# Row-maximum scores from the high part of q alone, as pairs of 64-row matmuls

## What is computed

```
q = einsum('dc,bct->btd', Wq, init) + bq        # init = context, d = 64 channels
k = einsum('dc,bct->bdt', Wk, init) + bk
R = einsum('btd,bds->bts', q, k)                # 1024 queries x 1024 keys
attention = softmax(R)                          # over the keys
v = einsum('oc,bct->bto', Wv, x) + bv
out = einsum('bts,bsc->bct', attention, v)
x = x + out                                     # x is layer-normed on its way in
```

## Time and profile before

| | |
|---|---|
| median of 3 runs | 2455.48 us (2455.11 to 2458.72) |
| profiled execution: span of its instructions | 2449.9 us |
| the median over that span (launch and end, and the spread of runs) | 5.6 us |
| TensorE matmuls busy | 2257.1 us (92%) |
| VectorE busy | 1900.4 us (78%) |
| ScalarE busy | 1128.1 us (46%) |
| GpSimd busy | 837.1 us (34%) |
| mean granted TensorE clock | 0.980 |
| HBM read and written | 81.74 MB and 16.78 MB, 40 GB/s |

### The profile page before, as it was taken

The page is one execution under the profiler, slowest core; times in us unless marked ns, Lnnn a source line. Parts: engine busy times, 40 slices in busy tenths (PEclk is TensorE's granted clock), DMA queues, the critical chain, the costliest instruction groups (busy, mean ns, idle before and its releaser), DMA issues.

```text
span 2449.9 us, 34700 instructions
## 1 busy us (share of the span) xinstructions
PE 2257.1 (92%) x11359; PEld 1749.3 (71%) x11359; DVE 1900.4 (78%) x2972; ACT 1128.1 (46%) x1657; POOL 837.1 (34%) x520
## 2 busy tenths in 40 slices
PE   0997999999999999999999999999999999999986
PEld 0775777777777777777777777777777777777764
DVE  1437788888888888888888888888888888888873
ACT  1104444555554544555554544545554544555541
POOL 0003333344344333344344333344344333334430
PEclk7999999999999999999999999999999999999996
DMA  8001011011011011011011011011011011011000
GB/s 230 9 1 52 18 44 39 30 43 43 26 43 43 34 43 43 26 43 43 26 43 43 34 43 43 26 43 43 26 43 43 36 41 43 26 43 43 30 22 26
DMA packets 45417, 98.86 MB, mean 40 GB/s; under 512 B 13968, under 2 KB 22544, under 8 KB 45392
## 3 DMA queue, kind: packets, MB, share of 16 engines
q1 hardware_dynamic: 33504, 96.48, 11.3%
q10 hardware_dynamic: 11888, 2.05, 0.5%
HBM read 81.74 MB, written 16.78 MB: 40 GB/s over the span
## 4 chain that ended last, share of the span: by engine, by line
PE 65%; DVE 14%; issue 10%; ACT 3%; POOL 0%; DVEq 0%; ACTq 0%; DMA 0%; SPq 0%; POOLq 0%
PE acc L1056 9%; PE acc L1095 8%; PE shared L1014 6%; PE scores L1039 5%; DVE p_lo L900 5%; DVE c_hi L924 3%; PE shared L1227 2%; PE acc L1052 2%; PE acc L1053 2%; PE shared L1164 2%; PE acc L1054 2%; PE shared L1112 2%; PE scores L1026 2%; PE shared L1180 2%; PE scores L1192 2%
## 5 line engine op out<-in xcount | busy, mean ns | idle before, releaser
L634 POOL TENSOR_TENSOR p_sum<-p_sum,prob 128x1024 f32<-128x1024 f32 x192 | 506.2, 2636 | 127.7 <-ACT prob L698 121.9
L900 DVE TENSOR_TENSOR p_lo<-prob,p_hi 128x1024 fp32r<-128x1024 f32 x256 | 353.4, 1381 | 83.8 <-ACT p_hi L705 82.3
L793 DVE TENSOR_REDUCE neg_max<-scores 128x1 f32<-128x1024 f32 x256 | 312.0, 1219 | 72.8 <-PE scores L1039 70.9
L615 POOL TENSOR_TENSOR rstd<-var_eps,minus_half 128x1 f32<-128x1 f32 x128 | 127.2, 994 | 665.4 <-DVE var_eps L787 662.1
L698 ACT ACTIVATE prob<-scores 128x1024 f32<-128x1024 f32 x256 | 260.3, 1017 | 199.8 <-PE scores L1084 180.6
L705 ACT ACTIVATE p_hi<-prob 128x1024 fp32r<-128x1024 f32 x256 | 271.2, 1059 | 76.4 <-PE acc L1095 72.3
L631 POOL TENSOR_TENSOR p_sum<-prob 128x1024 f32<-128x1024 f32 x32 | 85.7, 2677 | 642.5 <-ACT prob L698 642.5
L1095 PE MATMUL acc<-p_hi,v_hi 128*128 128x512 f32 x512 | 176.6, 426 | 94.6 <-DVE p_lo L900 94.6
L1056 PE MATMUL acc<-m_whole,cT_whole 128*128 128x512 f32 x512 | 255.2, 600 | 0.0
L1039 PE MATMUL scores<-k_hh,q_hl 128*128 128x512 f32 x512 | 212.5, 496 | 0.2 <-DVE k_l L802 0.2
L1069 PE MATMUL shared<-signT,y_hi 128*128 128x512 f32 x512 | 206.5, 403 | 0.4 <-ACT oscale L687 0.4
(11 more groups left out here) (230 smaller groups left out, 4873.4 us busy)
## 6 DMA issues: line engine op xcount, KB each, us to landing
c_in<-in_ctx SPq DMA_DIRECT2D x32, 512.0 KB, 3.3
xn<-in_x SPq DMA_DIRECT2D x32, 512.0 KB, 4.1
x<-in_x SPq DMA_DIRECT2D x32, 512.0 KB, 3.3
c_val<-in_ctx SPq DMA_DIRECT2D x32, 512.0 KB, 3.5
out_x<-oscale SPq DMA_DIRECT2D x32, 512.0 KB, 2.9
wq_nat<-in_L_xattn_Wq SPq DMA_DIRECT2D x4, 1024.0 KB, 10.2
wf_first<-in_L_ffn_weight SPq DMA_DIRECT2D x1, 2048.0 KB, 17.9
m_whole<-in_L_ffn_weight SPq DMA_DIRECT2D x1, 2048.0 KB, 22.8
```

The lines of the kernel that those rows point to most:

```text
L634: nc.gpsimd.tensor_tensor(p_sum[:, :], p_sum[:, :], prob[s % 2][:, :], ALU.add).then_inc(p_summed, 1)
L793: nc.vector.tensor_reduce(neg_max[:, DQK + t:DQK + t + 1], scores[(t + 1) % 2][:, :], AX_X, ALU.max, negate=True).then_inc(row_max, 1)
L900: nc.vector.tensor_tensor(p_lo[s % 2][:, :], prob[s % 2][:, :], p_hi[s % 2][:, :].bitcast(F32), ALU.subtract).then_inc(p_lo_ready, 1)
```

## The change

The row-maximum scores are now q high times k high alone. The term q low times k high is left out of them; the scores of the exponentials (L1083, L1084) keep all their parts. With 64 channels that product has 64 rows. The pair of a tile is laid out so that the left keys (half 0) come from partitions 0-63, with `q_hl`, and the right keys (half 1) from partitions 64-127, with a new `q_m`, whose partitions 64-127 hold the high part of q. In the built program the first matmul has a tile of 64 rows and 128 columns at array position (0, 0), the second one at (64, 0). All other matmuls of the loop keep tiles of 128 rows. For this, `q_m` and `k_l1` have 128 partitions: the maxima and the ones in 0-7, zeros in 8-63, and q high and k low in 64-127. The transpose L1135 turns 8 columns, which makes it a tile of 128 rows and 32 columns. Each matmul of a pair now increments the semaphore, and the maximum waits for both. Line numbers after L776 grow by three or less.

```diff
-        q_hm = sb("q_hm", [DQK + T, D], F32R)
+        q_m = sb("q_m", [P, D], F32R)
-        k_l1 = sb("k_l1", [DQK + T, D], F32R)
+        k_l1 = sb("k_l1", [P, D], F32R)
-        neg_max = sb("neg_max", [P, DQK + T])
+        neg_max = sb("neg_max", [P, T])
...
-                            nc.scalar.activation(q_hm[0:DQK, half(h)], scores[0][0:DQK, half(h)], ACT.Identity,
-                                                 bias=bq_col[0:DQK, :]).then_inc(q_hi_ready, 1)
+                            nc.scalar.activation(q_m[DQK:P, half(h)], scores[0][DQK:P, half(h)], ACT.Identity,
+                                                 bias=bq_col[DQK:P, :]).then_inc(q_hi_ready, 1)
...
-                nc.vector.memset(k_l1[DQK:DQK + T, :].bitcast(F32), 1.0).then_inc(const_made, 1)
-                nc.vector.memset(neg_max[:, :], 0.0).then_inc(const_made, 1)
+                nc.vector.memset(k_l1[0:DQK, :].bitcast(F32), 0.0).then_inc(const_made, 1)
+                nc.vector.memset(q_m[0:DQK, :].bitcast(F32), 0.0).then_inc(const_made, 1)
                 nc.vector.memset(route3[:, :].bitcast(F32), 0.0).then_inc(const_made, 1)
                 dve.wait_ge(const_made, 3)
+                nc.vector.memset(k_l1[0:T, :].bitcast(F32), 1.0).then_inc(const_made, 1)
+                dve.wait_ge(const_made, 4)
...
-                    dve.wait_ge(maxscores_done, nth(8, a, t + 1))
+                    dve.wait_ge(maxscores_done, nth(16, a, 2 * t + 2))
...
-                    nc.vector.scalar_tensor_tensor(k_l1[0:DQK, half(h)], scores[1][0:DQK, half(h)], bk_col[0:DQK, :],
+                    nc.vector.scalar_tensor_tensor(k_l1[DQK:P, half(h)], scores[1][DQK:P, half(h)], bk_col[DQK:P, :],
...
-                    for h in range(2):
-                        last = mm(scores[(t + 1) % 2][:, half(h)], q_hl[:, t * P:(t + 1) * P], k_hh[:, half(h)], start=True, stop=True)
-                    last.then_inc(maxscores_done, 1)
+                    rows = (slice(0, DQK), slice(DQK, P))
+                    for h, q in enumerate((q_hl, q_m)):
+                        mm(scores[(t + 1) % 2][:, half(h)], q[rows[h], t * P:(t + 1) * P], k_hh[rows[h], half(h)],
+                           start=True, stop=True).then_inc(maxscores_done, 1)
...
-                        last = mm(scores[s % 2][:, half(h)], k_l1[:, s * P:(s + 1) * P], q_hm[:, half(h)], start=False, stop=True)
+                        last = mm(scores[s % 2][:, half(h)], k_l1[:, s * P:(s + 1) * P], q_m[:, half(h)], start=False, stop=True)
...
-                        nc.tensor.transpose(scores[0][0:DQK + T, 0:P], neg_max[:, 0:DQK + T], ident[:, :]).then_inc(max_turned, 1)
+                        nc.tensor.transpose(scores[0][0:T, 0:P], neg_max[:, :], ident[:, :]).then_inc(max_turned, 1)
```

More of the change, by code:

```diff
@@ L789, in row_maximum @@
                 def row_maximum(a, t):
-                    dve.wait_ge(maxscores_done, nth(8, a, t + 1))
+                    dve.wait_ge(maxscores_done, nth(16, a, 2 * t + 2))
                     dve.wait_ge(max_turned, nth(1, a - 1, 1))
-                    nc.vector.tensor_reduce(neg_max[:, DQK + t:DQK + t + 1], scores[(t + 1) % 2][:, :], AX_X, ALU.max,
+                    nc.vector.tensor_reduce(neg_max[:, t:t + 1], scores[(t + 1) % 2][:, :], AX_X, ALU.max,
                                             negate=True).then_inc(row_max, 1)
@@ L801, in key_remainder @@
                     dve.wait_ge(k_hi_ready, nth(2, b, h + 1))
-                    nc.vector.scalar_tensor_tensor(k_l1[0:DQK, half(h)], scores[1][0:DQK, half(h)], bk_col[0:DQK, :],
-                                                   k_hh[0:DQK, half(h)].bitcast(F32), ALU.add,
+                    nc.vector.scalar_tensor_tensor(k_l1[DQK:P, half(h)], scores[1][DQK:P, half(h)], bk_col[DQK:P, :],
+                                                   k_hh[DQK:P, half(h)].bitcast(F32), ALU.add,
                                                    ALU.subtract).then_inc(k_ready, 1)
@@ L882, in body @@
                             nc.vector.tensor_tensor(
-                                q_hm[DQK:DQK + T, half(h)].rearrange("r (t j) -> r t j", t=4),
-                                scores[0][DQK:DQK + T, 0:P].unsqueeze(1).to_broadcast([T, 4, P]),
-                                ident[DQK:DQK + T, DQK + 4 * h:DQK + 4 * h + 4].unsqueeze(2).to_broadcast([T, 4, P]),
+                                q_m[0:T, half(h)].rearrange("r (t j) -> r t j", t=4),
+                                scores[0][0:T, 0:P].unsqueeze(1).to_broadcast([T, 4, P]),
+                                ident[0:T, 4 * h:4 * h + 4].unsqueeze(2).to_broadcast([T, 4, P]),
                                 ALU.mult).then_inc(max_ready, 1)
@@ L1007, in _ @@
                 mm = nc.tensor.matmul
-                pe.wait_ge(const_made, 3)
+                pe.wait_ge(const_made, 4)
                 def transposes(h, src, semaphore):
```

## The result

The changed kernel takes 2509.06 us in the median of four runs (2507.89 to 2515.74), the kernel before 2455.38 us. The ratio is 1.0221, with a 95% interval of 1.0207 to 1.0236: slower by 53.7 us. The profiled execution is the run of 2515.74 us, with a span of 2513.9 us, 64.0 us over the 2449.9 us of before.

The account below looks back on a forecast made before the run. TensorE was taken to bound the kernel, busy throughout the 17.53 us row-maximum stage. 256 pairs x 0.15 us gave 38.4 us, all on the path and everything else at nothing: 2455.5 became 2494 us, range 2412 to 2522.

Parts of the forecast that it names:

- the likeliest case: Row-maximum stage: pairs side by side, TensorE drained at each mode change; +0.15 us a pair, 2494 us, chance 0.45.
- the changes of mode: L1039 pairs: going from 128-row to 64-row matmuls and back costs 0.15 us net per pair, 38.4 us for 256.
- The pair runs side by side.: L1039: two 64-row matmuls on different array rows run concurrently; the second costs nothing at best, 0.234 us at worst.
- Emptying at a change of mode.: Around each L1039 pair: next weight load starts 0.07 us before the recorded end, 0.33 us after a matmul's start.
- The open loads.: Around each L1039 pair: weight loads not hidden at mode changes, taken as 0.10 us each.
- the distance over a pair should be 0.85 us: Sign in the later profile: from the matmul before an L1039 pair to the one behind, 0.85 us against 0.70 before.
- All of it on the path.: Row-maximum stage has no slack: all 38.4 us lengthen the run, 1.2 us an iteration; VectorE only idles more.
- the free rival: Row-maximum stage: mode changes free, pairs side by side, VectorE then sets the end; 40 us faster, 2415, chance 0.25.
- Everything else is priced at nothing.: ScalarE's q_m and VectorE's k_l1 writes, L1084's 128 rows, L1135's 8 columns, extra increments and hidden memsets cost nothing.
- The second stretch of the earlier trace: Exponentials and weighting of the values, after the row-maximum stage: forecast unchanged at 31.0 us.
- The rule of the Trainium skill on tiling modes: L1039 pairs: changing the tiling mode, not just the tile, drains TensorE; two drains per pair, speaking against the change.

Follow-up runs that it names:

- layout alone: Changed kernel with 128-row matmuls for the row maxima again, new layout and both increments kept: 2463.86 us against 2458.69 for the kernel before, ratio 1.0028.

## Why the prediction was right, and where it was not

The direction, the mechanism and the range held: 2494 us forecast, 2509 measured, within 2412 to 2522 and also within the likeliest case's own 2480 to 2522. The loss of 53.7 us comes apart into 1.19 x 32 = 38 us for the changes of mode, where 38.4 were forecast, 0.24 x 31 = 7 us for the copies and the wait, and some 8 us that are left, which I put down to the clock. The last two terms the forecast did not have; that they fit into its range is luck. With the clock's fall and the counted wait removed the program takes 2493.96 us. That this equals the forecast to 0.1 us is partly chance: some 3 us for ScalarE's copies, which the forecast priced at nothing, are still in it.

- *The pair runs side by side.* Taken as the bound without a row, and right: both start within 0.01 us, and putting them on the same rows costs 0.22 us per pair.
- *Emptying at a change of mode.* The setup rows gave 0.07 us before the recorded end; the loop shows 0.08. From the matmul ahead to the pair's load it is 0.32 us, forecast 0.33.
- *The open loads.* Counted at 0.10 us each, with both loads of the pair at once. From the pair to the next load it is 0.43 us as worked out. The stage grew by 1.11 us; the emptying ahead of its first pair lies in the rest, and with it the eight pairs cost 1.19 / 8 = 0.149 us each, where 0.15 was forecast. One sign of the forecast was misread: "the distance over a pair should be 0.85 us" is 0.74 us from start to start. The records of the pair and of the matmul behind it begin with their open loads, so the last 0.10 us shows behind that start and not ahead of it.
- *All of it on the path.* Right: TensorE is busy for the whole stage, and VectorE only idles longer. The end of the stage was TensorE's; the free rival, in which VectorE sets it, needed changes of mode that cost nothing. Grouping showed its idea from the other side: with pairs two at a time TensorE did wait for VectorE within the stage.
- *"Everything else is priced at nothing."* This step failed. It holds for the memsets, the 128-row second operand, the column tile of L1138 and the increment on TensorE. It does not hold for the copies to partitions from 64 on (0.13 us more between starts, of which 0.11 to 0.14 us an iteration reaches the path) nor for the wait that counts by 16 (0.16 us ahead of one p_lo per iteration). With the emptying ahead of the first pair (0.08 us), which belongs to the changes of mode, they make the 0.32 us of the rest, 10 us in all; taken one by one they come to a little more. The second stretch of the earlier trace rows was unchanged, as forecast: up to there TensorE's instructions lie where they lay, within 0.1 us; all of this comes behind it, in a part of the iteration for which I had forecast nothing. I had looked at shapes and counts, not at how the neighbours overlap.
- *The clock.* The granted clock was 1.00 in the stretch before, and the forecast kept it there without a word. It fell at the fourth pair in 11 iterations of the profiled run, 16.5 us, and by their mean clock in fewer in the others. This is a term that the forecast lacked. The Trainium skill, TensorE: Matmul & The Clock Gate, Part 1, says that activity releases the throttle and that its lack brings it back. The trace agrees as to the level, 0.51 of full speed in the stretch shown, but TensorE is recorded busy in all of the stretches before it. The stretches before the fall hold the short router matmuls and the pairs with their emptyings; with 128-row pairs in the same order it did not fall, and moving one unit removed it. Which of the two weighs how much was not separated, and with other orders the clock fell without 64-row pairs.
- *The rule of the Trainium skill on tiling modes* (TensorEngine Tiling (Array Packing), Key Properties) held for the number of rows: at a change the next load began only 0.08 us before the recorded end, and a second pair in the same mode did not pay again. For the number of columns the setup rows had disagreed with it, and behind L1138, whose column tile changes, the next matmul starts after 0.03 us as it does behind L1135.

## What to carry to other kernels

Two 64-row matmuls side by side save one matmul's time (0.234 us with 512 columns here), and going into 64-row mode and out again costs about 0.37 us: two emptyings of 0.08 to 0.09 us and two weight loads of 0.10 us that nothing hides. So a lone pair between 128-row matmuls loses 0.14 us. Two pairs in a row gain 0.10 by this count, and 0.13 us was measured at the group that waited for nothing; over a whole stage of four groups only 0.05 us came of it (17.73 against 17.78 us), since one group waited for VectorE. Longer runs in one mode were not tried. Price a change of operand layout by the starts of the neighbouring instructions, and after every change look at the granted clock per stage: moving one unit of the changed kernel was worth some 10 us, and another order of the kernel before cost 60 us, 33 of them by the clock.

## What the runs showed that I had not expected

- ScalarE's copies of equal length start 0.57 us apart when all begin at partition 0, and 0.70 us apart when every second one begins at partition 64.
- The form of a counted wait can cost the engine 0.16 us elsewhere in its program: with a count of 8 per batch p_lo starts 0.18 us behind the reciprocal, with 16 per batch 0.34 us, in each of the thirteen kernels profiled. In the second case VectorE's sequencer has an ALU_OP of 40 ns for another wait of the loop (L900), which it lacks in the first.
- Two matmuls that end together and increment the same semaphore let the waiting VectorE start 0.07 us behind their recorded end, where one increment gives 0.04 us, as do two from matmuls one behind the other (layout alone).
- In a program whose TensorE is recorded busy for all of a stage, the granted clock can still fall to the lower level once per iteration, for 1.5 us of loss each time. It fell in 11 of 31 iterations of the changed kernel and in none with one unit of its matmuls moved.
